# Keys of two context chunks in one matmul of 500 columns, and new fill tables for the prologue and the last batch

## The chip, the cores and the metric

The kernel runs on one core of a Trainium2 chip, as one launch. The metric is the device time in microseconds, median of several runs. Engines are named as in the profile: PE is TensorE, ACT is ScalarE, DVE is VectorE, POOL is GpSimd, SP is SyncE, which issues most DMAs.

## The reference

```python
def xattn(query, key, value, Wq, Wk, Wv, Wo):      # 16 heads of 32
    q = (query @ Wq.T).reshape(B, L, H, D) * scale
    k = (key @ Wk.T).reshape(B, -1, H, D)
    v = (value @ Wv.T).reshape(B, -1, H, D)
    scores = sigmoid(einsum('blhd,bshd->bhls', q, k))
    o = einsum('bhls,bshd->blhd', scores, v).reshape(B, L, E)
    return o @ Wo.T

x = x + tanh(g_xattn) * xattn(layernorm(x), ctx, ctx, ...)    # x (16, 224, 512), ctx (16, 750, 512)
x = x + tanh(g_ffn) * ffn(layernorm(x), w1, b1, w2, b2)       # 8 experts of 2048, gelu, 448 tokens each
```

## The kernel before, in words

**Arithmetic.** Every large product is made of three products of split operands: an operand is stored as a high part (HI, rounded to the matmul's format) and a low part (LO, the rest), and `three_terms` adds HI·HI, HI·LO and LO·HI over four blocks of 128 rows. One fill is therefore 12 matmuls into one PSUM bank. ACT makes the HI part, DVE the LO part.

**Batches.** `batches` runs the body for b = -1 (prologue), 0 to 15 (the 16 batches) and 16 (tail); all are unrolled. A body has 12 steps s. In step s PE computes the scores of step s (`scores`: 8 matmuls of 224 columns, a head group of four heads mt = s // 3 against a third of the context s % 3), ACT turns them into `probs` by one sigmoid, and PE meanwhile does the fills that the table of this batch lists for this step. `scores_ps` is single, so the scores of step s+1 wait for the sigmoid of step s. Twice a batch, at steps 0 and 6, `heads` multiplies six steps of probabilities by the values (48 short matmuls).

**Fills** have a kind and a number. K: keys of context chunk c = j % 3 for head group j // 3, where j = (i + 6) % 12 is the step that will use them; 250 columns. V: values, 512 columns. Q: queries, 224 columns. O: output projection, 512 columns. U and T: transposes. S: transpose of the layernorm moments into a row. The tables are `FILL` (batches 1 to 14), `FILL_FIRST` (prologue), `FILL_0` (batch 0) and `FILL_LAST` (batch 15). All engines walk the same table: PE fills the bank, ACT and DVE take it out (`leave`), POOL stores K, Q, U and S results to DRAM scratch in table order. Fill number g of a table uses bank g % 3 of `fill_ps` and waits until the fill that held that bank has left it.

**Keys and queries** go through DRAM to be laid out again: `store_k` writes one K fill (250 KB) to `k_scr`, a ring of six places with a semaphore `s_k_st` for each, and `gather_k(n, j)` on SP reads it back in three DMAs into one of three places of `k_st`, two steps ahead, once the scores of step j-3 are done. The same holds for `store_q` and `gather_q`.

**SP is one queue** and each of its waits holds everything behind it. Two places matter here. At the prologue's end `load_xT(1)` waits for the stored row of moments (`s_stat_st`) and then reads it back as `x_mr`; `gather_k(0, 2)` stands behind it. In the last batch, at step 5, `load_w1(0, 1)` loads the second piece of the first expert's weights into `k_stage` (the buffer from which `store_k` writes) and waits for that until all keys are stored; `gather_k` for step 8 stands behind it.

```python
if known(e, 0) and c == 1:
    for r in range(RING):
        alone(sp, s_k_st[r], 16 * 2 * B)
```

**Last batch.** No later batch has to be prepared, so `HIDDEN_AT` puts the first expert's hidden products (`hidden`, in halves of 6 matmuls of 448 columns) into the steps from 8 on; its numbers count steps of batch 15, and 12 is step 0 of the tail. After the tail's `heads` come the two O fills, into `scores_ps`.

**Experts.** After the tail, 8 experts of 8 chunks run in `expert`; the change touches nothing in them.

Of the kernel before, what the change touches and what calls it, by code (L numbers as in the profile page):

```python
# [10 lines left out]
F32 = mybir.dt.float32  # L11
# [25 lines left out]
def flamingo_block(nc, io, scr, out):  # L37
# [27 lines left out]
    FILL = [(1, "K", 0), (1, "O", 0), (2, "K", 1), (2, "O", 1), (3, "K", 2), (3, "V", 2), (3, "U", 0), (3, "U", 1),  # L65
# [3 lines left out]
    FILL_FIRST = [(0, "K", 6), (1, "T", 0), (1, "T", 1), (2, "Q", 0), (3, "Q", 1), (4, "K", 7), (5, "K", 8), (6, "K", 9),  # L69
                  (7, "V", 0), (8, "K", 10), (9, "K", 11), (9, "S", 1)]  # L70
    FILL_0 = [(0, "Q", 6), (0, "Q", 7), (1, "K", 0), (1, "V", 7), (2, "K", 1), (2, "V", 2), (3, "K", 2),
              (3, "V", 3), (4, "K", 3), (4, "V", 4), (5, "V", 5)] + [f for f in FILL if f[0] > 5]
    FILL_LAST = [(0, "K", 0), (0, "K", 1), (1, "K", 2), (1, "O", 0), (1, "V", 2), (2, "K", 3), (2, "V", 3),
                 (3, "K", 4), (3, "V", 4), (4, "V", 5), (5, "O", 1), (7, "K", 5), (8, "S", 0), (9, "U", 0), (10, "U", 1)]
# [47 lines left out]
    def nth(kind, b, i):  # L122

        if kind == "K":
            return K_FIRST[i] if known(b, -1) else STEPS * b + AHEAD + i + 1
        if kind == "S":
            return 1 if i == 1 else b + 2
        return {"V": 6, "Q": KT, "T": 2, "O": 2, "U": 2}[kind] * target(b, kind, i) + tile_of(kind, i) + 1

    def tile_of(kind, i):  # L130

        return i % KT if kind == "Q" else i % 6 if kind == "V" else i

# [49 lines left out]
    with ExitStack() as ctx:  # L183
# [133 lines left out]
        def _(sp):  # L317
# [107 lines left out]
            def load_w1(e, c):  # L425
# [82 lines left out]
        def _(pool):  # L508
# [14 lines left out]
            def store_k(b, i):  # L523
# [3 lines left out]
                at(pool, s_k_in[(j - RING) % 3], 16 * COPIES * (4 * n + (j - RING) // 3 + 1))  # L527
                own(pool)
                pool.dma_start(scr["k"][j % RING].rearrange("h p s -> p h s"), k_stage[:, j % 3].bitcast(F32)  # L529
                               ).then_inc(s_k_st[j % RING], 16)  # L530
# [25 lines left out]
            for r in range(RING):  # L556
                pool.wait_ge(s_k_st[r], 16 * 2 * B)
# [5 lines left out]
        def _(pe):  # L563
# [61 lines left out]
            def fill(b, kind, i):  # L625
# [149 lines left out]
        def _(act):  # L775
            def ctx_hi(n, h, par, c):
                act.wait_ge(s_ctx_in[chunk_place(par, c)], 16 * (chunk_round(h, par, c) + 1))

                at(act, full["K"], STEPS * (n - 1) + 9 + c + 1)
# [26 lines left out]
            def leave(b, kind, i):  # L806
# [9 lines left out]
                elif kind == "K":  # L816
                    j = step_of(i)
                    at(act, s_k_st[(j - 3) % RING], 16 * (2 * n + (j - 3) // RING + 1))
                    nc.scalar.copy(k_stage[:, j % 3, HI, :], ps[:, 0:SC]).then_inc(hi["K"], 1)  # L819
# [25 lines left out]
            def body(b, h, par):  # L845
                nh, npar = (h, 1) if par == 0 else (h + 1, 0)
                for s in range(STEPS):
# [26 lines left out]
                    if known(b, B - 1):  # L874
# [4 lines left out]
                        if s == 8:  # L879
# [18 lines left out]
            def e_hi(e, m, c):  # L898
# [335 lines left out]
```

## Time and profile before

| | us |
|---|---|
| median of 3 runs | 1717.65 (1716.29 to 1717.78) |
| profiled execution, its own time | 1717.5 |
| its span in the trace | 1716.0 |
| PE busy | 1690.3 (99%), 12525 matmuls |
| ACT busy | 777.0 (45%) |
| DVE busy | 682.3 (40%) |
| POOL busy | 210.2 (12%) |
| DMA engines, mean busy share | 63% of the span |

A matmul's duration in the trace overlaps with the next one's; what a fill costs PE is the distance from its start to the start of what follows. The profiled execution lies 0.15 us under the median. Its own time is 1.5 us more than its span.

### The profile page before, as it was taken

The page shows a single profiled execution, that of the slowest core. Times are in us where ns is not written, and L with a number is a line of the kernel's source. Part 1 is how long each engine was busy: PE and PEld are TensorE (multiplying, and loading weights), DVE is VectorE, ACT ScalarE, POOL GpSimd, SP SyncE. Part 2 cuts the span into 40 slices and gives each one's busy share as a digit, 9 for nine tenths or more (in the row PEclk, how much of TensorE's full clock was granted, in tenths as well). Part 3 has the DMA queues.
Part 4 walks back from the last instruction along what each step waited for, and adds up shares of the span by engine and source line. Part 5 has one row for each costly group of instructions (what it writes and reads, how often), then busy time and mean ns, then how long its engine had stood idle before and what let it go on. Part 6 is the DMA issues. An engine that isn't in the chain of part 4 may idle for free. (4 is left out here: it accounts for less than half of the span.)

```text
span 1716.0 us, 32304 instructions
## 1 busy us (share of the span) xinstructions
PE 1690.3 (99%) x12525; PEld 1510.3 (88%) x12525; DVE 682.3 (40%) x1139; ACT 777.0 (45%) x975; POOL 210.2 (12%) x303
## 2 busy tenths in 40 slices
PE   8999999999999999999999996999999999999999
PEld 7888888888888888898888885899999999999998
DVE  5323322332332232233233223355556464555554
ACT  4545555545555545455455443434333333333332
POOL 1122122122122121122121120000000000000000
PEclk9999999999999999999999998999999999999999
DMA  7887687686687686787786683545263535435351
GB/s 243 232 235 206 186 236 202 180 236 196 190 237 201 193 237 201 199 230 190 202 233 190 197 226 101 159 139 191 104 206 107 183 130 165 154 117 186 101 175 59
DMA packets 199651, 315.53 MB, mean 184 GB/s; under 512 B 25368, under 2 KB 152672, under 8 KB 199520
## 3 DMA queue, kind: packets, MB, share of 16 engines
q1 hardware_dynamic: 176176, 236.05, 49.5%
q0 software_dynamic: 23344, 77.68, 13.0%
q8 instruction: 88, 1.44, 0.4%
q14 instruction: 43, 0.35, 0.1%
HBM read 235.06 MB, written 78.58 MB: 183 GB/s over the span
## 5 line engine op out<-in xcount | busy, mean ns | idle before, releaser
L795 ACT ACTIVATE probs<-scores_ps 125x1792 f32<-125x1792 f32 x192 | 320.4, 1669 | 152.4 <-PE scores_ps L602 122.4
L756 PE MATMUL scores_ps<-ctx_hl,wK 128*128 128x448 f32 x1536 | 316.7, 362 | 0.4 <-ACT st_row L826 0.4
L756 PEld LDWEIGHTS scores_ps<-ctx_hl,wK 128*128 128x128 f32 x1536 | 288.0, 188 | 20.4 <-issue 0.6
L570 PE MATMUL fill_ps<-ctx_hl,wK 128*128 128x250 f32 x2304 | 297.9, 281 | 1.0 <-DVE wK L955 1.0
L570 PEld LDWEIGHTS fill_ps<-ctx_hl,wK 128*128 128x128 f32 x2304 | 280.0, 189 | 7.0 <-issue 5.7
L570 PE MATMUL fill_ps<-wV,ctx_hl 128*125 128x512 f32 x1152 | 281.1, 395 | 0.0
L570 PEld LDWEIGHTS fill_ps<-wV,ctx_hl 128*125 128x125 f32 x1152 | 207.9, 185 | 46.6
L736 PE MATMUL fill_ps<-wQ,wV 128*128 128x448 f32 x1152 | 245.7, 368 | 0.4 <-DVE wV L1109 0.4
L529 POOL DMA_DIRECT2D k_scr<-k_stage x192 | 139.2, 725 | 792.1 <-DVE k_stage L1037 597.5
L736 PEld LDWEIGHTS fill_ps<-wQ,wV 128*128 128x128 f32 x1152 | 217.5, 189 | 18.1 <-DVE wV L1109 0.6
L602 PEld LDWEIGHTS scores_ps<-q_st,k_st 96*125 96x125 f32 x1536 | 191.9, 190 | 30.2 <-DMA k_st<-k_scr 13.9
L602 PE MATMUL scores_ps<-q_st,k_st 96*125 96x224 f32 x1536 | 203.2, 275 | 14.2 <-DMA k_st<-k_scr 13.4
L1037 DVE TENSOR_TENSOR k_stage<-fill_ps,k_stage 128x250 fp32r<-128x250 f32 x192 | 79.9, 416 | 287.5 <-ACT k_stage L819 286.8
L619 PE MATMUL heads_ps<-probs,v_sb 125*32 125x224 f32 x3072 | 151.9, 353 | 0.0
L843 ACT COPY v_sb<-fill_ps 125x512 f32<-125x512 f32 x96 | 56.3, 586 | 195.1 <-PE fill_ps L570 195.1
L619 PEld LDWEIGHTS heads_ps<-probs,v_sb 125*32 125x32 f32 x3072 | 96.6, 110 | 45.5 <-issue 0.3
L924 ACT ACTIVATE q_stage<-fill_ps,b_sb 128x448 f32<-128x448 f32 x96 | 60.8, 635 | 143.1 <-PE fill_ps L736 143.0
L949 DVE TENSOR_TENSOR ctx_hl<-ctx_raw,ctx_hl 128x1000 fp32r<-128x1000 f32 x48 | 57.6, 1200 | 165.7 <-ACT ctx_hl L781 165.7
L1120 DVE CAST ctx_hl<-q_stage 128x896 fp32r<-128x896 f32 x64 | 40.1, 627 | 162.4 <-ACT q_stage L924 162.4
L570 PE MATMUL fill_ps<-xnT,wQ 128*128 128x224 f32 x768 | 96.6, 279 | 0.2 <-DVE wQ L955 0.2
L570 PEld LDWEIGHTS fill_ps<-xnT,wQ 128*128 128x128 f32 x768 | 91.8, 195 | 0.7 <-DVE wQ L955 0.4
L819 ACT CAST k_stage<-fill_ps 128x250 fp32r<-128x250 f32 x192 | 69.8, 363 | 41.3 <-PE fill_ps L570 41.3
(85 smaller groups left out, 1274.0 us busy)
## 6 DMA issues: line engine op xcount, KB each, us to landing
k_st<-k_scr SPq DMA_DIRECT2D x576, 125.0 KB, 3.8
v_sb<-w_in SPq DMA_DIRECT2D x94, 512.0 KB, 4.5
k_scr<-k_stage POOLq DMA_DIRECT2D x192, 250.0 KB, 4.7
ctx_raw<-ctxT_in SPq DMA_DIRECT2D x48, 500.0 KB, 5.7
q_st<-q_scr SPq DMA_DIRECT2D x192, 112.0 KB, 3.4
probs<-w_in SPq DMA_DIRECT2D x32, 512.0 KB, 3.8
x_res<-x_in SPq DMA_DIRECT2D x32, 448.0 KB, 4.3
q_scr<-q_stage POOLq DMA_DIRECT2D x64, 224.0 KB, 5.6
```

The source lines that it names most:

```text
L529: pool.dma_start(scr["k"][j % RING].rearrange("h p s -> p h s"), k_stage[:, j % 3].bitcast(F32)).then_inc(s_k_st[j % RING], 16)
L570: last = pe.matmul(out_, lhsT(kt, a), rhs(kt, c), start=(kt == 0 and t == 0), stop=(kt == KT - 1 and t == 2))
L602: last = pe.matmul(scores_ps[0:ST, j, t * L:(t + 1) * L], k_st3[:, r, j, t * ST:(t + 1) * ST], q_st3[:, slot, j, :], start=True, stop=True)
L619: last = pe.matmul(heads_ps[j * HD:(j + 1) * HD, cols], v_sb[0:ST, v_place(par, 2 * pair + t), mt * P + j * HD:mt * P + (j + 1) * HD], pro ...
L736: last = pe.matmul(hid_ps[bank][:, 0:T], w1[:, slot, a, kt, k * P:(k + 1) * P], xt[:, d, kt, :], start=(kt == 0 and t == 0), stop=(kt == K ...
L756: last = pe.matmul(y_ps[:, dt, 0:T], w2[:, slot, a, k, dt * P:(dt + 1) * P], hid_hl[:, slot, d, k, :], start=(c == 0 and k == 0 and t == 0 ...
L795: nc.scalar.activation(probs[0:ST, s % VISIT], scores_ps[0:ST, :, 0:2 * L], ACT.Sigmoid, scale=SCALE).then_inc(s_probs, 1)
L819: nc.scalar.copy(k_stage[:, j % 3, HI, :], ps[:, 0:SC]).then_inc(hi["K"], 1)
L843: nc.scalar.copy(v_sb[0:ST, v_place(1 - par if i < 2 else par, i % 6), :], fill_bank(b, "V", i)[0:ST, :]).then_inc(done["V"], 1)
L924: nc.scalar.activation(hid[:, k, :], hid_ps[2 * (c % 2) + k][:, 0:T], ACT.Gelu_apprx_tanh, bias=b1[:, 2 * c + k:2 * c + k + 1]).then_inc(s ...
L949: nc.vector.tensor_tensor(ctx_chunk(c, LO), ctx_raw[:, chunk_place(par, c)], ctx_chunk(c, HI).bitcast(F32), ALU.subtract).then_inc(s_ctx_l ...
L1037: nc.vector.tensor_tensor(k_stage[:, j, LO, :], ps[:, 0:SC], k_stage[:, j, HI, :].bitcast(F32), ALU.subtract).then_inc(done["K"], 1)
```

## The change

1. `is_pair(b, i)`: from batch 0 on, a K fill with i % 3 == 0 covers chunks 0 and 1 of the context for its head group. Its 12 matmuls have 500 columns: the moving operand is read in two pieces of 250 that lie 2000 elements apart, and 2000 bytes of a bank are written in one piece. One ACT cast and one DVE subtraction take 500 columns out, and one POOL DMA of 500 KB stores both ring places. Fills with i % 3 == 1 are gone (except K 7 and K 10 in the prologue, which keeps single fills); chunk 2 keeps its own fill of 250 columns.
2. A pair's store signals only the semaphore of its first ring place; `ring_sem` and `keys_done` give the new numbers. A pair's store waits for the gathers from both places that it overwrites.
3. K 5 moves from step 7 to 6, K 8 from 9 to 8, and with them the splitting of the next context's chunks (`CTX_SPLITS`) from steps 5, 6, 7 to 4, 5, 7.
4. The two Q fills of batch 0, step 0, move into the prologue, step 9, ahead of S.
5. In the last batch `load_w1(0, 1)` goes to `ctx_raw` and waits for the split tokens (`s_xt_lo`) instead of the keys. Its split moves from step 8 to 7. O 1 moves from step 5 to 3, K 5 from 7 to 6, S from 8 to 9, U 0 and U 1 from 9 and 10 to 8 and 9, and the hidden halves start at step 7.

```diff
-    FILL = [(1, "K", 0), (1, "O", 0), (2, "K", 1), (2, "O", 1), (3, "K", 2), (3, "V", 2), (3, "U", 0), (3, "U", 1),
-            (4, "K", 3), (4, "V", 3), (5, "V", 4), (5, "V", 5), (6, "K", 4), (7, "K", 5), (7, "K", 6), (7, "Q", 0),
-            (8, "K", 7), (8, "V", 0), (9, "K", 8), (9, "K", 9), (9, "S", 0), (9, "Q", 1), (10, "K", 10), (10, "V", 1),
-            (11, "K", 11), (11, "Q", 2), (11, "Q", 3)]
+    FILL = [(1, "K", 0), (1, "O", 0), (2, "O", 1), (3, "K", 2), (3, "V", 2), (3, "U", 0), (3, "U", 1), (4, "K", 3),
+            (4, "V", 3), (5, "V", 4), (5, "V", 5), (6, "K", 5), (7, "K", 6), (7, "Q", 0), (8, "K", 8), (8, "V", 0),
+            (9, "K", 9), (9, "S", 0), (9, "Q", 1), (10, "V", 1), (11, "K", 11), (11, "Q", 2), (11, "Q", 3)]
...
-                  (7, "V", 0), (8, "K", 10), (9, "K", 11), (9, "S", 1)]
...
+                  (7, "V", 0), (8, "K", 10), (9, "K", 11), (9, "Q", 2), (9, "Q", 3),
+                  (9, "S", 1)]
...
-    FILL_LAST = [(0, "K", 0), (0, "K", 1), (1, "K", 2), (1, "O", 0), (1, "V", 2), (2, "K", 3), (2, "V", 3),
-                 (3, "K", 4), (3, "V", 4), (4, "V", 5), (5, "O", 1), (7, "K", 5), (8, "S", 0), (9, "U", 0), (10, "U", 1)]
...
+    FILL_LAST = [(0, "K", 0), (1, "K", 2), (1, "O", 0), (2, "V", 2), (3, "K", 3), (3, "O", 1),
+                 (3, "V", 3), (4, "V", 4), (5, "V", 5), (6, "K", 5), (8, "U", 0), (9, "U", 1), (9, "S", 0)]
...
-    CTX_SPLITS = {5: 0, 6: 1, 7: 2}
...
-    HIDDEN_AT = {8: [(0, 0, 0), (0, 0, 1)], 9: [(0, 1, 0)], 10: [(0, 1, 1)], 11: [(1, 0, 0)], 12: [(1, 0, 1)]}
+    CTX_SPLITS = {4: 0, 5: 1, 7: 2}
...
+    HIDDEN_AT = {7: [(0, 0, 0)], 8: [(0, 0, 1)], 9: [(0, 1, 0)], 10: [(0, 1, 1)], 11: [(1, 0, 0), (1, 0, 1)]}
...
+    def is_pair(b, i):
+        return b > -1 and i % 3 == 0
...
+    def ring_sem(n, j):
+        return j % RING if n == 0 and j < AHEAD else j % RING - (j % 3 == 1)
...
-                return x_raw[:, 0:HALF] if c == 0 else k_stage[:].rearrange("p r h s -> p (r h s)")[:, 0:HALF].bitcast(F32)
+                return x_raw[:, 0:HALF] if c == 0 else ctx_raw[:].rearrange("p r s -> p (r s)")[:, 0:HALF]
...
                 if known(e, 0) and c == 1:
-                    for r in range(RING):
-                        alone(sp, s_k_st[r], 16 * 2 * B)
+                    alone(sp, s_xt_lo, 2)
...
+                at(pool, s_k_in[(j + 1 - RING) % 3], 16 * COPIES * (4 * n + (j + 1 - RING) // 3 + 1))
                 own(pool)
-                pool.dma_start(scr["k"][j % RING].rearrange("h p s -> p h s"), k_stage[:, j % 3].bitcast(F32)
-                               ).then_inc(s_k_st[j % RING], 16)
+                pool.dma_start(scr["k"][j % RING:j % RING + 2].rearrange("r h p s -> p (r h) s"),
+                               k_stage[:, 0:2].rearrange("p r h s -> p (r h) s").bitcast(F32)
+                               ).then_inc(s_k_st[ring_sem(n, j)], 16)
...
+                    if is_pair(b, i):
+                        last = three_terms(ps[:, 0:2 * SC], lambda kt, a: w["K"][:, a, kt, mt * P:(mt + 1) * P],
+                                           lambda kt, a: ctx_hl[:, 0:2, a, kt, :])
...
-                        if s == 8:
+                        if s == 7:
                             e_hi(0, 1, 1)
```

**PE where batch 0 begins.** S of the prologue is the row with `mv`. Before:

```order
L570 MATMUL fill_ps<-ctx_hl,wK 128x250 x24
L674 MATMUL fill_ps<-ident,mv 8x112
L602 MATMUL scores_ps<-q_st,k_st 125x224 x8
L570 MATMUL fill_ps<-xnT,wQ 128x224 x24
L602 MATMUL scores_ps<-q_st,k_st 125x224 x8
L570 MATMUL fill_ps<-ctx_hl,wK 128x250 x12
L570 MATMUL fill_ps<-wV,ctx_hl 125x512 x12
L602 MATMUL scores_ps<-q_st,k_st 125x224 x8
```

Changed:

```order
L589 MATMUL fill_ps<-xnT,wQ 128x224 x24
L697 MATMUL fill_ps<-ident,mv 8x112
L621 MATMUL scores_ps<-q_st,k_st 125x224 x8
L589 MATMUL fill_ps<-wV,ctx_hl 125x512 x12
L621 MATMUL scores_ps<-q_st,k_st 125x224 x8
L589 MATMUL fill_ps<-ctx_hl,wK 128x500 x12
L621 MATMUL scores_ps<-q_st,k_st 125x224 x8
```

The queries now stand ahead of S; between S and the scores of step 2 (the third row of scores) there is one V fill and one pair, where two Q, one K and one V fill stood.

**POOL at the same place**, the stores of the prologue. Before:

```order
L529 DMA k_scr<-k_stage 128x2x250 [waits done_K]
L520 DMA q_scr<-q_stage 128x2x224 [waits done_Q] x2
L529 DMA k_scr<-k_stage 128x2x250 [waits done_K] x5
L545 DMA stat_scr<-st_row 4x2x112 [waits done_S]
L520 DMA q_scr<-q_stage 128x2x224 [waits done_Q] x2
```

Changed:

```order
L542 DMA k_scr<-k_stage 128x2x250 [waits done_K]
L532 DMA q_scr<-q_stage 128x2x224 [waits done_Q] x2
L542 DMA k_scr<-k_stage 128x2x250 [waits done_K] x5
L532 DMA q_scr<-q_stage 128x2x224 [waits done_Q] x2
L564 DMA stat_scr<-st_row 4x2x112 [waits done_S]
```

The two query stores now stand between the last key store and the store of the moments.

**PE in the changed last batch**, from the scores of step 7 to the end of its `heads`; `x_res` is U and `mv` is S:

```order
L621 MATMUL scores_ps<-q_st,k_st 125x224 x8
L759 MATMUL fill_ps<-wQ,wV 128x448 x6
L621 MATMUL scores_ps<-q_st,k_st 125x224 x8
L701 MATMUL fill_ps<-ident,x_res 128x112 x4
L759 MATMUL fill_ps<-wQ,wV 128x448 x6
L621 MATMUL scores_ps<-q_st,k_st 125x224 x8
L701 MATMUL fill_ps<-ident,x_res 128x112 x4
L697 MATMUL fill_ps<-ident,mv 8x112
L759 MATMUL fill_ps<-wQ,wV 128x448 x6
L621 MATMUL scores_ps<-q_st,k_st 125x224 x8
L759 MATMUL fill_ps<-wQ,wV 128x448 x6
L621 MATMUL scores_ps<-q_st,k_st 125x224 x8
```

U 1 and S now stand in one step, next to each other, and both use bank 2; before, S, U 0 and U 1 had a step each (8, 9 and 10).

## Rows read from the trace of the kernel before

**Rows 1.** Whom PE waited for: total us, times, longest us.
```profile
PE scores_ps L602 <- DMA k_st<-k_scr: 13.4, 1, 13.4
PE fill_ps L674 <- DVE mv L31: 3.3, 1, 3.3
```

**Rows 2.** Stretches: length, then each engine's busy us, PE clock, DMA share, GB/s.
```profile
35.00:41.60 6.60, 6.60 (x34) 6.56 (x35) 0.67 (x2) 3.64 (x5) 1.91 (x3) 0.54 0.30 95
...
229.39:294.96 65.57, 65.57 (x588) 57.27 (x587) 20.32 (x45) 33.92 (x43) 12.78 (x18) 1.00 0.73 209
...
1016.27:1093.08 76.81, 62.62 (x576) 51.05 (x574) 17.98 (x35) 32.81 (x36) 6.98 (x10) 0.89 0.50 132
```

**Rows 3.** PE in order of time, batch 2: start us, us, what, count.
```profile
205.05 2.94 PE L570 MATMUL fill_ps<-ctx_hl,wK 128*128 128x250 f32 x24
207.83 1.50 PE L570 MATMUL fill_ps<-xnT,wQ 128*128 128x224 f32 x12
209.16 1.04 PE L602 MATMUL scores_ps<-q_st,k_st 96*125 96x224 f32 x8
210.04 1.57 PE L570 MATMUL fill_ps<-ctx_hl,wK 128*128 128x250 f32 x12
211.44 2.94 PE L570 MATMUL fill_ps<-wV,ctx_hl 128*125 128x512 f32 x12
214.22 1.03 PE L602 MATMUL scores_ps<-q_st,k_st 96*125 96x224 f32 x8
```

**Rows 4.** The chain that ended last, experts: start us, us, matmuls of 448 columns.
```profile
1142.18 4.81 PE scores_ps L756 x24
```

**Rows 5.** Last batch, SP's queue and PE in order of time, [idle before <- releaser].
```profile
1066.10 0.35 SPq L436 DMA_DIRECT2D k_stage<-w_in  x1
1066.60 1.27 SPq L333 DMA_DIRECT2D k_st<-k_scr  x3
...
1072.38 2.02 PE L602 MATMUL scores_ps<-q_st,k_st 96*125 96x224 f32 x8 [13.37 <-DMA k_st<-k_scr]
...
1081.71 1.11 PE L602 MATMUL scores_ps<-q_st,k_st 96*125 96x224 f32 x8 [0.23 <-ACT probs L795]
...
1084.67 1.11 PE L602 MATMUL scores_ps<-q_st,k_st 96*125 96x224 f32 x8 [0.23 <-ACT probs L795]
...
1086.93 4.75 PE L619 MATMUL heads_ps<-probs,v_sb 125*32 125x224 f32 x96
...
1093.08 5.76 PE L570 MATMUL scores_ps<-wO,oT 128*112 128x512 f32 x24
```

**Rows 6.** ACT between the sigmoids of steps 9, 10 and 11 of the last batch.
```profile
1082.86 1.67 ACT L795 ACTIVATE probs<-scores_ps 125x1792 f32<-125x1792 f32 x1 [0.87 <-PE scores_ps L602]
1084.42 0.53 ACT L836 COPY x_raw<-fill_ps 128x448 f32<-128x448 f32 x1
```

**Rows 7.** Prologue's end, PE in order of time.
```profile
34.98 0.34 PE L674 MATMUL fill_ps<-ident,mv 112*8 112x112 f32 x1 [3.35 <-DVE mv L31]
...
36.89 4.85 PE L570 MATMUL fill_ps<-xnT,wQ 128*128 128x224 f32 x24
```

**Rows 8.** Prologue's end, DVE, POOL, SP's queue and PE's weight loads in order of time.
```profile
34.86 0.42 DVE L1037 TENSOR_TENSOR k_stage<-fill_ps,k_stage 128x250 fp32r<-128x250 f32 x1
...
36.55 0.61 POOL L545 DMA_DIRECT2D stat_scr<-st_row  x1
...
39.49 0.83 SPq L392 DMA_DIRECT2D x_mr<-stat_scr  x2
...
40.41 1.33 SPq L333 DMA_DIRECT2D k_st<-k_scr  x3
...
46.70 0.95 PEld L602 LDWEIGHTS scores_ps<-q_st,k_st 96*125 96x125 f32 x8 [0.34 <-DMA k_st<-k_scr]
```

**Rows 9.** Issue to landing of those three gathers, and of batch 3's store of moments.
```profile
DMA to landing us min/median/max: 4.3/4.5/5.4
...
DMA to landing us min/median/max: 4.2/4.2/4.2
```

More of the change, by code:

```diff
@@ L124, in nth @@
         if kind == "K":
-            return K_FIRST[i] if known(b, -1) else STEPS * b + AHEAD + i + 1
+            return K_FIRST[i] if known(b, -1) else K_FILLS * b + AHEAD + i - (i + 1) // 3 + 1
         if kind == "S":
@@ L527, in store_k @@
                 at(pool, s_k_in[(j - RING) % 3], 16 * COPIES * (4 * n + (j - RING) // 3 + 1))
+                if not is_pair(b, i):
+                    own(pool)
+                    pool.dma_start(scr["k"][j % RING].rearrange("h p s -> p h s"), k_stage[:, j % 3].bitcast(F32)
+                                   ).then_inc(s_k_st[ring_sem(n, j)], 16)
+                    return
+                at(pool, s_k_in[(j + 1 - RING) % 3], 16 * COPIES * (4 * n + (j + 1 - RING) // 3 + 1))
                 own(pool)
[L529 to L530 removed]
+                pool.dma_start(scr["k"][j % RING:j % RING + 2].rearrange("r h p s -> p (r h) s"),
+                               k_stage[:, 0:2].rearrange("p r h s -> p (r h) s").bitcast(F32)
+                               ).then_inc(s_k_st[ring_sem(n, j)], 16)
             def body(b, h, par):
@@ L556, in _ @@
             for r in range(RING):
-                pool.wait_ge(s_k_st[r], 16 * 2 * B)
+                pool.wait_ge(s_k_st[r], 16 if r % 3 == 1 else 16 * 2 * B)
             for mt in range(KT):
@@ L817, in leave @@
                     j = step_of(i)
-                    at(act, s_k_st[(j - 3) % RING], 16 * (2 * n + (j - 3) // RING + 1))
-                    nc.scalar.copy(k_stage[:, j % 3, HI, :], ps[:, 0:SC]).then_inc(hi["K"], 1)
+                    last = 2 * n + (j - 3) // RING + 1
+                    if last > 0:
+                        m, k = (n, j - 3) if j > 2 else (n - 1, j - 3 + STEPS)
+                        act.wait_ge(s_k_st[ring_sem(m, k)], 16 * last)
+                        if is_pair(b, i) and ring_sem(m, k + 1) != ring_sem(m, k):
+                            act.wait_ge(s_k_st[ring_sem(m, k + 1)], 16 * last)
+                    if is_pair(b, i):
+                        nc.scalar.copy(k_stage[:, 0:2, HI, :], ps[:, 0:2 * SC].rearrange("p (r s) -> p r s", s=SC)
+                                       ).then_inc(hi["K"], 1)
+                    else:
+                        nc.scalar.copy(k_stage[:, j % 3, HI, :], ps[:, 0:SC]).then_inc(hi["K"], 1)
                 elif kind == "Q":
@@ L902, in e_hi @@
                 if known(e, 0) and c == 0:
-                    act.wait_ge(full["V"] if m == 1 else full["K"], (6 if m == 1 else 12) * B)
+                    act.wait_ge(full["V"] if m == 1 else full["K"], 6 * B if m == 1 else keys_done(B - 1, STEPS - 1))
                 if m == 1:
@@ L1036, in leave @@
                     j = step_of(i) % 3
-                    nc.vector.tensor_tensor(k_stage[:, j, LO, :], ps[:, 0:SC], k_stage[:, j, HI, :].bitcast(F32),
-                                            ALU.subtract).then_inc(done["K"], 1)
+                    if is_pair(b, i):
+                        nc.vector.tensor_tensor(k_stage[:, 0:2, LO, :], ps[:, 0:2 * SC].rearrange("p (r s) -> p r s", s=SC),
+                                                k_stage[:, 0:2, HI, :].bitcast(F32), ALU.subtract).then_inc(done["K"], 1)
+                    else:
+                        nc.vector.tensor_tensor(k_stage[:, j, LO, :], ps[:, 0:SC], k_stage[:, j, HI, :].bitcast(F32),
+                                                ALU.subtract).then_inc(done["K"], 1)
                 elif kind == "Q":
@@ L1117, in split_hidden @@
                 if known(e, 0) and c == 0:
-                    dve.wait_ge(full["K"], 12 * B)
+                    dve.wait_ge(full["K"], keys_done(B - 1, STEPS - 1))
                     dve.wait_ge(full["V"], 6 * B)
```

21 lines of the change are left out of this document (13 added, 8 removed).

## The prediction, made before the changed kernel ran

> **What bounds the kernel now.** I read the busy times first (the table above): PE is busy in 99% of the span, no other engine in half of it. Then the waits of PE [rows 1]: in the whole span it waits for little else than two things, once 13.4 us for gathered keys and once 3.3 us for the moments. Then the stretches [rows 2]. An ordinary batch lasts 65.57 us and PE is busy in all 65.57 of it, at full clock. So an ordinary batch gets shorter only if the matmuls themselves cost less; what ACT, DVE, POOL and the DMA queues save there is worth nothing unless it was late. The first and the last batch are different: there the clock column falls to 0.54 and 0.89, the two waits lie there, and the order of SP's and POOL's queues sets the time. I price the three places apart.
>
> **Ordinary batches: the pair.** Starts to starts in batch 2 [rows 3]: 24 key matmuls of 250 columns in 207.83 - 205.05 = 2.78 us; 12 alone in 211.44 - 210.04 = 1.40; 12 value matmuls of 512 columns in 214.22 - 211.44 = 2.78, so 232 ns each. In the experts 24 matmuls of 448 columns take 4.81 us [rows 4], 200 ns each. No row has 500 columns. 500 columns at the full 2.4 GHz are 208 ns. What a matmul takes over its columns is 14 ns at 448 (200 - 187), 19 at 512 (232 - 213) and 12 to 13 at 250. So 500 columns should take 222 to 227 ns; I take 224, nearer to the 448 row, since keys are multiplied as the experts' weights are, with 128 stationary columns. A pair then takes 12 x 224 = 2.69 us, where two fills took 2.78 (together) to 2.80 (apart, and a little more where other work stands between). I take a gain of 0.12 us a pair, between 0.05 and 0.17. There are 4 pairs in each of batches 0 to 14, without the first of batch 0, which goes into the prologue's sum: 59 x 0.12 = **7.1 us less** (3 to 10).
>
> What no row shows is a moving operand read in two pieces, and what that costs. Bounded from above by the price of two separate starts: then a pair is as dear as 24 matmuls in 2.78 and the gain is nearly nil. From below by columns alone, 12 x 208 = 2.50 us, a gain of 0.3 a pair or 18 us. I stay at 0.12, since the break comes once in 250 columns.
>
> The Trainium skill (TensorE: Matmul & The Clock Gate, Back-to-back issue gap) gives N/2.4 + 2.5 ns for a warm matmul. By it a pair would save only 12 x 2.5 ns = 0.03 us, and all pairs 1.8 us. The rows disagree with the page: 232 ns at 512 columns, not 216 [rows 3].
>
> What else moves in an ordinary batch I cost at nothing. Steps 2 and 10 keep one fill of 2.78 us; the sigmoid loop needs scores start to scores start 2.96 us (1084.67 - 1081.71, where it did bind) [rows 5], and 0.87 + 2.78 = 3.65 covers it. ACT's and DVE's 500 columns lie beside the next fill. The cover of the bigger store is the two steps between a store and its gather, over 7 us. The context split starts a step earlier, behind the two chunks' last K fill, which is now at step 4; it lies beside the 5.6 us of two V fills. The Q fills and S keep their places. If this cover failed, a late gather would show as a PE wait for `k_st` in every batch; 1.1 us a batch would eat all gain outside the prologue.
>
> **Last batch.** Here one wait sets the time. SP stood at the load into `k_stage` until 1066.10, and the gather for step 8 was issued behind it at 1066.60 [rows 5]. PE waited 13.37 us, then ran at half clock for some time: step 8's scores at 1072.38 took 2.02 us, not 1.03. From this batch's first scores to the O fills of the tail is 1093.08 - 1016.27 = 76.8 us.
>
> The changed load waits for the split tokens, which come before step 5's scores, so SP issues it at once and the next gather as soon as its slot is free. I built the new row of work from the same prices: heads 4.67 + 0.1, V, O 2.78 each, pair 2.69, K 1.40 to 1.53, scores 0.87 to 0.97. Step 0: 8.4 us; 1: 5.0; 2: 3.7; 3: 9.1; 4: 3.7, and 0.5 of wait, because the cast of the tokens again stands ahead of sigmoid 4; 5: 3.7; 6: 7.1. So step 7's scores start 41.2 us after the first. Steps 7 and 8 have less work than the sigmoid loop and cost 2.96 each. Step 9 has a **new wait**: U 1 and S are neighbours and use the same bank, so S waits until ACT has taken U 1 out, and ACT does that after sigmoid 9. From the scores' start: sigmoid starts after 1.15, takes 1.6, U's copy 0.53 [rows 6], so S starts at 3.3, and the hidden half behind it ends at 4.7, not 2.6. Step 9 costs 4.7, step 10 2.96, step 11 0.9 + 2 x 1.25 = 3.4. That is 41.2 + 5.9 + 4.7 + 3.0 + 3.4 = 58.2 to `heads`, and from `heads` to the O fills 1093.08 - 1086.93 = 6.15 as before (no hidden half covers the split of the last outputs now, but its own 1.5 us is gone too). 64.4 against 76.8: **12.4 us less**. The tail behind it starts from the same events and keeps its length. Bounds: 14.5 without the new wait and the one at step 5; 11 if the last keys (K 5, stored about 1.5 us after their fill, landing some 3 us later, gathered in 5) come 1.5 us late for step 11, which by my row of work they just do not.
>
> **Prologue.** Before, PE stood 3.35 us ahead of S [rows 7] and ran the next 6 us at half clock (0.54 [rows 2]): the two Q fills of batch 0 took 4.7 us where 24 such matmuls take 2 x 1.33 = 2.7 [rows 3, 7]. The change puts these Q fills into the gap. S now waits for the bank of K 11, whose subtract ends at 34.86 + 0.42 = 35.28 [rows 8], so S comes 0.3 us later, at about 35.4, but after an idle of 1.1 us, not 3.35. If that were all, 1.4 + 2.7 + 3 us of half clock would mean 5 to 6 us less.
>
> But step 2's scores did not wait for PE even before: the weight load at 46.70 is marked as waiting for the gather [rows 8]. That gather is behind `x_mr` on SP, which is behind the stored moments: stored at 36.55, `x_mr` at 39.49, gather at 40.41, landed at 46.70 [rows 8]. In POOL's new order the two query stores (0.73 each) come ahead of the moments: 36.55 + 1.5 = 38.0. Their landing took 2.9 us alone (39.49 - 36.55) and 4.2 beside key and query stores [rows 9]; now it has 700 KB of stores ahead of it, so I take 4.2: `x_mr` at 42.3, the gather at 43.2, its third DMA 0.9 later and 5.4 us to land [rows 9]: step 2's scores at **48.9** (47.2 to 49.6), 2.2 us later than before. PE reaches this point, with one V fill and one pair since S, at 35.4 + 0.9 + 2.8 + 0.1 + 0.9 + 2.7 = 42.9. It then stands 6 us, longer than the 3.35 that were followed by the low clock before, so I expect the same again: half of some 6 us, 3 us lost. Ahead of 48.9 PE has done one K fill more than before (1.4 us), and the gather of step 3, a step behind on SP, comes perhaps 0.5 late. The sum is 2.2 - 1.4 + 3.0 + 0.5, less about 0.8 because part of the half clock falls on PE's waits for the sigmoid: **3.5 us more** (1.6 less to 6 more).
>
> **Sum.** 1717.5 - 7.1 - 12.4 + 3.5 = 1701.5, against its own 1717.5; the profiled run is 0.15 from the median, which I let go. Experts: the same work, no change.
>
> **Rivals.**
> (a) *The prologue is really mended*: the moments land in 2.9 us and the gather in 4, or the stall comes without low clock. Then the prologue gives 1 to 5 us instead of costing 3.5: 1693 to 1697. For it: the first gather there landed in 4.3. Against: the gather was already late by 0.34 [rows 8].
> (b) *Pairs bring nothing*, since a matmul's extra time grows with its columns (12 ns at 250, 19 at 512): then only the last batch counts, 1717.5 - 1.8 - 12.4 + 3.5 = 1707.
> (c) *Slower*: the moving operand in two pieces is read more slowly, as a stall of the array at each break. The place is every pair fill. It decides from 8.9 / (59 x 12) = 12.6 ns over the 234 of two separate matmuls, so from 247 ns for 500 columns; at 265 ns, 30 ns above that price a matmul, it is 1717.5 - 8.9 + 59 x 12 x 0.031 = 1731. For it: no row of this trace reads so. Against it: within a piece the columns are neighbours as before, and only one step in 500 is long. The Trainium skill (SBUF — State Buffer, Door 1: The DMA port swizzle) says that an access which crosses to a new line of 16 bytes pays; by that one long step costs what a quarter of all steps cost anyway, and (c) would not happen.
> (d) *The last batch keeps part of its wait*, because something else on SP is late there, the keys of K 5 or the first expert's tokens: 5 to 8 us of the 12.4 stay, 1707 to 1710.
>
> **How the numbers follow.** Forecast as summed (1698 to 1704): 0.55. (a) 0.15, (b) 0.12, (c) 0.07, (d) 0.11. The bounds of the terms give 1717.5 - 10 - 14.5 - 1.6 = 1691 at one end and 1717.5 - 3 - 11 + 6 = 1709.5 at the other; joint extremes are rare. From 1693 to 1710 all of the forecast and nearly all of (a), (b) and (d) lie inside. A difference under 0.2% (3.4 us) can't be told from none. Above 1721 lies most of (c), 0.06; between 1714 and 1721 the rest of (c) and a sum of bad ends of (d), 0.03; below is 0.91.
>
> **What would show it.** In the trace of the changed kernel: 12 key matmuls of 500 columns from start to start 2.69 us (2.78 or more is (b), 2.97 or more is (c)); an ordinary batch of 65.1 us; in the last batch no wait above 2 us, one of about 2 us before S in step 9, and full clock throughout; from its first scores to the tail's O fills 64 us; in the prologue a wait of 4 to 6 us for `k_st` ahead of step 2's scores, then a stretch at half clock, with `x_mr` issued after 41. I would be wrong in kind if PE waited for `k_st` in ordinary batches, or if the experts changed.

## The result, and the profile of the changed kernel

The changed kernel takes 1748.95 us (median of 4 runs, 1745.25 to 1753.60), the kernel before 1716.99 (4 runs). The ratio is 1.0186, with a 95% interval from 1.0166 to 1.0206: 32 us slower, where 16 us faster was forecast. The profiled execution took 1751.64 us with a span of 1749.8, 33.8 more than the span before.

What PE waits for, in the changed kernel (engine, tile and line, releaser, us in total, times, longest):

```profile
PE fill_ps L589 <- DVE ctx_hl L982: 27.2, 15, 1.8
PE scores_ps L621 <- DMA k_st<-k_scr: 5.0, 1, 5.0
PE fill_ps L697 <- ACT x_raw L869: 1.8, 1, 1.8
PE scores_ps L621 <- ACT probs L819: 1.8, 4, 0.6
...
PE scores_ps L589 <- DVE oT L1055: 1.4, 1, 1.4
```

The first row has no counterpart in [rows 1]. It stands in each of 15 batches, and it is no gather: PE waits for the low part of the next context. Here are two of the fifteen on PE's timeline, in two different batches (start us, us, then in brackets the idle time before and its releaser):

```profile
80.44 1.04 PE L621 MATMUL scores_ps<-q_st,k_st 96*125 96x224 f32 x8
83.29 1.64 PE L589 MATMUL fill_ps<-ctx_hl,wK 128*128 128x250 f32 x12 [1.81 <-DVE ctx_hl L982]
84.77 2.94 PE L589 MATMUL fill_ps<-wV,ctx_hl 128*125 128x512 f32 x12
87.55 1.03 PE L621 MATMUL scores_ps<-q_st,k_st 96*125 96x224 f32 x8
...
488.83 1.04 PE L621 MATMUL scores_ps<-q_st,k_st 96*125 96x224 f32 x8
491.68 2.67 PE L589 MATMUL fill_ps<-ctx_hl,wK 128*128 128x250 f32 x12 [1.81 <-DVE ctx_hl L982]
494.15 3.50 PE L589 MATMUL fill_ps<-wV,ctx_hl 128*125 128x512 f32 x12
497.48 1.04 PE L621 MATMUL scores_ps<-q_st,k_st 96*125 96x224 f32 x8
```

The waits are equal, what follows is not. Behind the first, the K fill takes 1.48 us from start to start and the V fill 2.78. Behind the second they take 2.47 and 3.33: the granted clock had fallen to its lower level, 1.2 GHz, and this costs 1.5 us more. It happened in 9 of the 15 batches.

The fill at 83.29 is K 8, the keys of the third context chunk of the **next** batch for head group 0; the first fill that reads a chunk waits for its split into HI and LO. That chunk was split by ACT (80.89) and DVE (81.94), ahead of the sigmoid of this step:

```profile
80.89 1.03 ACT L805 CAST ctx_hl<-ctx_raw 128x1000 fp32r<-128x1000 f32 x1
81.81 1.67 ACT L819 ACTIVATE probs<-scores_ps 125x1792 f32<-125x1792 f32 x1
```
```profile
81.94 1.20 DVE L982 TENSOR_TENSOR ctx_hl<-ctx_raw,ctx_hl 128x1000 fp32r<-128x1000 f32 x1 [0.53 <-ACT ctx_hl L805]
```

In the kernel before, the same split stood at the same place, and K 8 (the first 12 of the 24 matmuls) came 3.2 us after its end, behind K 7, V 0 and the scores of step 9 [rows 3]:

```profile
210.66 1.20 DVE L949 TENSOR_TENSOR ctx_hl<-ctx_raw,ctx_hl 128x1000 fp32r<-128x1000 f32 x1 [0.53 <-ACT ctx_hl L781]
```
```profile
215.09 2.97 PE L570 MATMUL fill_ps<-ctx_hl,wK 128*128 128x250 f32 x24
```

The stretches (from, to, length, busy time and count of PE, PEld, DVE, ACT, POOL, granted clock, DMA share, GB/s) are a batch with a fall of the clock, a batch without one, and everything from the O fills of the tail to the end. Under them the same last stretch of the kernel before:

```profile
102.17:171.03 68.86, 67.05 (x539) 56.52 (x538) 19.89 (x42) 33.95 (x39) 9.98 (x14) 0.98 0.72 199
171.03:238.34 67.31, 65.50 (x538) 55.02 (x538) 19.89 (x41) 33.96 (x39) 9.97 (x14) 1.00 0.73 204
1121.62:1749.80 628.18, 624.23 (x3069) 574.31 (x3069) 339.43 (x385) 217.83 (x269) 4.95 (x9) 1.00 0.44 145
```
```profile
1093.08:1716.00 622.92, 618.82 (x3070) 574.59 (x3069) 339.28 (x385) 217.93 (x269) 4.91 (x9) 1.00 0.45 146
```

[rows 2] had 65.57 us for a batch and 76.81 for the last. The last batch, from its first scores to the O fills, is now 1121.62 - 1057.24 = 64.38 us:

```profile
1057.24 1.03 PE L621 MATMUL scores_ps<-q_st,k_st 96*125 96x224 f32 x8
...
1107.80 0.26 PE L697 MATMUL fill_ps<-ident,mv 112*8 112x112 f32 x1 [1.79 <-ACT x_raw L869]
...
1121.62 3.70 PE L589 MATMUL scores_ps<-wO,oT 128*112 128x512 f32 x15 [1.40 <-DVE oT L1055]
```

**Where the 33.8 us came from**, by marks that both traces have. From the start to the `heads` of batch 0, step 6: 69.32, before 66.82, +2.5 (with one K fill of 1.4 us more done by then). From there to the last batch's first scores: 987.92, before 949.45, +38.5. The last batch: -12.4. From the O fills on: +5.3. The sum is 33.8 before rounding.

The 5.3 us at the end are not the change's. The experts' code is the same, and its hidden matmuls take 206.7 ns from start to start in this execution against 202.6 in the profile of before, at the same clock. Of the 13 profiles here eleven have 202.6, those of experiments 4 and 5 too, which only put work into the waits of the changed kernel, and two have 206.7, this one and that of experiment 9. The 29 executions of the kernel before lie in two groups, 17 from 1715.79 to 1717.87 us and 12 from 1719.03 to 1723.21. A difference of less than that needs several runs or a look at one place of the trace, and I compare places below.

### The profile page after: what moved, and what is told of

Same layout as the page of the kernel before. It is cut to its first block and busy times, and to the rows that moved or that the text cites. A ratio compares the mean times of both kernels' runs of the same rounds, so it can differ in the third digit from the quotient of the medians.

```text
span 1749.8 us, 30424 instructions
## 1 busy us (share of the span) xinstructions
PE 1704.0 (97%) x11781; PEld 1484.2 (85%) x11781; DVE 675.3 (39%) x1077; ACT 777.8 (44%) x913; POOL 166.9 (10%) x241
## 5 line engine op out<-in xcount | busy, mean ns | idle before, releaser
L589 PE MATMUL fill_ps<-ctx_hl,wK 128*128 128x500 f32 (+1 forms) x1560 | 299.0, 343 | 27.7 <-DVE ctx_hl L982 27.2
L589 PEld LDWEIGHTS fill_ps<-ctx_hl,wK 128*128 128x128 f32 x1560 | 243.9, 197 | 61.0 <-issue 35.6
L589 PE MATMUL fill_ps<-wV,ctx_hl 128*125 128x512 f32 x1152 | 286.0, 400 | 0.0
L589 PEld LDWEIGHTS fill_ps<-wV,ctx_hl 128*125 128x125 f32 x1152 | 213.9, 190 | 48.8
L1071 DVE TENSOR_TENSOR k_stage<-fill_ps,k_stage 128x500 fp32r<-128x500 f32 x62 | 42.1, 678 | 234.0 <-ACT k_stage L849 234.0
L542 POOL DMA_DIRECT2D k_scr<-k_stage x68 | 48.9, 719 | 516.6 <-DVE k_stage L1074 428.1
L589 PE MATMUL fill_ps<-wO,oT 128*112 128x512 f32 x360 | 88.0, 393 | 0.0
```

The lines of the kernel that those rows point to most:

```text
L589: last = pe.matmul(out_, lhsT(kt, a), rhs(kt, c), start=(kt == 0 and t == 0), stop=(kt == KT - 1 and t == 2))
L1071: nc.vector.tensor_tensor(k_stage[:, 0:2, LO, :], ps[:, 0:2 * SC].rearrange("p (r s) -> p r s", s=SC), k_stage[:, 0:2, HI, :].bitcast(F32) ...
```

## Experiments

The kernel before was run again beside each round of experiments, and the ratios are to these runs: its median was 1721.34 us (9 runs) for experiments 1, 4, 8 and 10, 1719.03 (9 runs) for 2, 6, 7 and 9, and 1717.12 (7 runs) for 3, 5 and 11. Differences between medians of different rounds are therefore rough.

**1. K 8 back at step 9**, all else as changed. The theory: the move of K 8 alone, and not pairs, stores or gathers, made the kernel slower.

```diff
-(7, "Q", 0), (8, "K", 8), (8, "V", 0), (9, "K", 9)
+(7, "Q", 0), (8, "V", 0), (9, "K", 8), (9, "K", 9)
```

> The changed kernel with one entry of FILL moved back: K 8 from step 8 to step 9, behind the split of the next context's third chunk at step 7, which it reads. Theory: the 15 waits of 1.8 us for that split, and the nine falls of the clock behind them, go; ordinary batches become 65.4 us (65.58 less four pairs at 0.05) and the median 1749 - 28.7 - 13.9 = 1706. If the slower hidden matmuls of the experts (39.04 us for half an expert, 38.68 in the kernel before) are a state of the run and not of the program, 1701. Rival, the larger stores delay something in ordinary batches: a batch stays over 66.5 us and the median above 1720.

Measured: 1704.79 us (4 runs; ratio to before 0.9908, 0.9876 to 0.9941), 44 us under the changed kernel. No wait for `ctx_hl` is left, and a batch is 65.22 us with PE busy in all of it:

```profile
101.07:166.29 65.22, 65.22 (x538) 54.93 (x537) 19.89 (x42) 33.87 (x39) 10.01 (x15) 1.00 0.77 210
```

Against the batches above this is 2.09 us for a wait of 1.81 and what it adds around it (15 batches: 31.3), and 1.54 more for each of 9 falls (13.9): 45.2 us for one entry of a table. Less the gain of the pairs, 5.2 us (below), and less 1.4, since the changed kernel had done one more K fill at the first mark, these are the 38.5 us between the marks, within 0.1.

**2. The split one step earlier, K 8 left at step 8.** The theory says that K 8 may stand at step 8 if its operand is there.

```diff
-    CTX_SPLITS = {4: 0, 5: 1, 7: 2}
+    CTX_SPLITS = {4: 0, 5: 1, 6: 2}
...
-                    if attends(b) and prepares(b) and s in (1, 2, 6):
-                        load_ctx(b + 1, nh, npar, {1: 0, 2: 1, 6: 2}[s])
+                    if attends(b) and prepares(b) and s in (1, 2, 5):
+                        load_ctx(b + 1, nh, npar, {1: 0, 2: 1, 5: 2}[s])
```

> The changed kernel with K 8 left at step 8, but the next context's third chunk loaded one step earlier (behind step 5 in place of 6) and split one step earlier (6 in place of 7). Theory (the 15 waits of 1.8 us for DVE ctx_hl and the falls of the clock behind them are the split's being one step late for K 8, and nothing else about the move): waits and falls gone, ordinary batches at 65.2 us, 1704 to 1706, as with K 8 at step 9. Rival (loading and splitting a step earlier meets the V fills' leaves or the chunk's buffer, and another wait takes its place): ordinary batches at 66 us or more, 1716 or above.

Measured: 1702.65 us (3 runs; 0.9908, 0.9881 to 0.9934). The batch, the split on DVE, and K 8 on PE with no idle time before it:

```profile
99.19:164.44 65.25, 65.25 (x538) 54.92 (x537) 19.89 (x42) 33.85 (x39) 9.98 (x14) 1.00 0.78 209
```
```profile
76.04 1.20 DVE L982 TENSOR_TENSOR ctx_hl<-ctx_raw,ctx_hl 128x1000 fp32r<-128x1000 f32 x1 [0.51 <-ACT ctx_hl L805]
```
```profile
80.35 1.56 PE L589 MATMUL fill_ps<-ctx_hl,wK 128*128 128x250 f32 x12
```

The split ends at 77.24, 3.1 us ahead of the fill. So the step at which the next context is split was the cause, and there was room to have it earlier.

**3. K 8 at step 8 in the kernel before**, and nothing else. Does the early K 8 cost as much without pairs?

```diff
-            (8, "K", 7), (8, "V", 0), (9, "K", 8), (9, "K", 9)
+            (8, "K", 7), (8, "K", 8), (8, "V", 0), (9, "K", 9)
```

> The kernel before with one edit: K 8 is done at step 8 behind K 7, not at step 9. Nothing else of the change is in it: no pairs, the old last batch and prologue. Theory (the loss of the changed kernel comes from K 8 alone, which reads the next context's third chunk a step before its split): PE waits 1 to 2 us for DVE ctx_hl in each of 15 batches, and the granted clock falls in some of them: 1717 + 15 to 27 for the waits, + up to 14 for the falls: 1735 to 1758. Rival (the wait needs the pairs or their new order of copies): no wait for ctx_hl, 1717 to 1722.

Measured: 1726.41 us (2 runs; 1.0053, 1.0033 to 1.0073), 9.3 above before, less than the theory expected. Its waits, and PE's timeline in batch 0:

```profile
PE fill_ps L570 <- DVE ctx_hl L949: 6.2, 15, 0.4
```
```profile
78.07 1.56 PE L570 MATMUL fill_ps<-ctx_hl,wK 128*128 128x250 f32 x12
80.05 1.63 PE L570 MATMUL fill_ps<-ctx_hl,wK 128*128 128x250 f32 x12 [0.41 <-DVE ctx_hl L949]
```

The wait is there in 15 batches, but of 0.4 us, since K 7 (78.07, 1.4 us) stands ahead of K 8 in the same step and covers the rest; the batch is 66.18 us and its clock never fell. The pair had taken K 7 out of step 8. So both parts of the change meet here: one brought K 8 forward, the other removed the work that would have hidden its wait. The expectation had missed this cover too.

**4 and 5. PE kept busy in the wait.** Is the fall of the clock caused by PE standing still? The changed kernel gets transposes of the identity (results unused) ahead of each K 8, first 13, then 5. They only fill the waiting for the operand: the batches keep their length (below).

```diff
+                        if not known(b, -1) and (kind, i) == ("K", 8):
+                            pe.wait_ge(s_o_lo, 2 * b + 1)
+                            turns(13)
```

> The changed kernel with 13 transposes of the identity on PE right ahead of each K 8 fill, in place of idling there; their result is used by nothing. Theory: the clock falls only because PE idles, so no fall is left in ordinary batches, the waits stay hidden behind the dummies, which must not be longer than the wait, and the median is 1749 - 14 = 1735. Rival, the clock falls for another reason (power, the DMA load): the falls stay and the median is 1749 or more.

> The changed kernel with 5 transposes of the identity ahead of each K 8, where an earlier kernel had 13. With 13, 0.4 us of each wait of 1.8 us were left as idle time, the clock never fell in an ordinary batch and the time was 1733.7 us; with none, 1.8 us were left, the clock fell in 9 of 15 batches and the time was 1749. With 5 about 1.3 us should be left. Theory (what makes the clock fall is how long PE stands): fewer falls than 9 or none: 1734 to 1744. Rival (any break at this place lets it fall, and the 13 transposes hid it otherwise): 9 falls or so, 1749.

With 13 the idle time left is 0.4 us in each batch, and the time 1733.72 us (2 runs). With 5 it is 1.26 us, and the time 1734.82 (2 runs). PE's timeline with 5:

```profile
81.65 0.71 PE L731 MATMUL heads_ps<-ident 128*128 128x128 f32 x5
83.62 1.64 PE L589 MATMUL fill_ps<-ctx_hl,wK 128*128 128x250 f32 x12 [1.26 <-DVE ctx_hl L985]
```

In neither did the clock fall in an ordinary batch; all their batches are 67.3 us, the length of the changed kernel's six batches without a fall. So 1.26 us of idle time left the clock up in all 15 batches, and 1.81 us did not in 9 of 15. The executions without a profile agree by their mean granted clock: 0.988 or 0.989 in all four of the changed kernel, 0.997 or 0.998 in all four of these two. The falls cost 1749 - 1734 = 15 us by the medians, and 9 x 1.54 = 13.9 by the batches. Why six of the fifteen were spared, with the same wait, stays open.

**6. Both chunks of a pair in one piece.** `ctx_hl` is laid out so that the 500 columns of the moving operand are neighbours; K 8 at step 9.

```diff
-        ctx_hl = sb("ctx_hl", [P, 3, 2, KT, SC], F32R)
+        ctx_hl = sb("ctx_hl", [P, 2, KT, 3, SC], F32R)
...
-                                           lambda kt, a: ctx_hl[:, 0:2, a, kt, :])
+                                           lambda kt, a: ctx_hl[:, a, kt, 0:2, :].rearrange("p c s -> p (c s)"))
```

> The kernel with K 8 back at step 9 (1704.8 us), with the split context laid out so that the two chunks of a fill of 500 columns lie in one piece (the moving operand has one run of 500 numbers, not two of 250 that are 2000 numbers apart). In that kernel's profile a fill of two chunks takes 2.75 us (229 ns a matmul) where 500/512 of the 232.5 ns of the 512-column matmuls would be 227. Theory (the break costs next to nothing): 2.75 us a pair still, time within 2 us. Rival (the break in the operand eats the gain): 2.69 us a pair, 59 x 0.06 = 3.5 us lower, 1701.

Measured: 1701.22 us (2 runs; 0.9896, 0.9860 to 0.9931). PE around a pair, in the kernel of experiment 1 and in this one:

```profile
498.04 2.91 PE L589 MATMUL fill_ps<-ctx_hl,wK 128*128 128x500 f32 x12
500.79 2.94 PE L589 MATMUL fill_ps<-wO,oT 128*112 128x512 f32 x12
```
```profile
494.79 2.88 PE L589 MATMUL fill_ps<-ctx_hl,wK 128*128 128x500 f32 x12
497.51 2.93 PE L589 MATMUL fill_ps<-wO,oT 128*112 128x512 f32 x12
```

A pair goes from 2.75 to 2.72 us, and a batch from 65.22 to 65.09:

```profile
98.58:163.67 65.09, 65.09 (x539) 54.95 (x538) 19.89 (x42) 33.84 (x39) 9.98 (x14) 1.00 0.77 210
```

Neither expectation is met exactly. The break costs 2 to 3 ns a matmul, 2 us in all batches, which is real in the trace and too small for two runs to show.

**7. The last batch's change alone, in the kernel before**: single K fills, old prologue. Against the kernel of experiment 8, which differs only in the pairs, it prices the pairs.

```diff
-                    for r in range(RING):
-                        alone(sp, s_k_st[r], 16 * 2 * B)
+                    alone(sp, s_xt_lo, 2)
```

(and `FILL_LAST`, `HIDDEN_AT`, the place in `ctx_raw` and the split at step 7, as in the change.)

> The kernel before with the last batch's change alone (S behind U 1 one step earlier, the first keys' load no longer behind the second half-batch, the new list of fills), its keys in single fills of 250 columns as before and its prologue as before. It does all that the kernel with the old prologue and K 8 at step 9 does (1702.8 us, span 1698.3), but for the pairs. Theory (last batch -12.4 us, a pair worth 0.05 us in its fill and the batch 0.35 us in all): 1717.5 - 12.4 = 1705, that is 3 to 6 us above the kernel with pairs. Rival (pairs are worth the 0.12 us of the prediction): 1709 to 1710. Rival (the last batch's gain needs the pairs): 1712 or more.

Measured: 1710.63 us (5 runs; 0.9952, 0.9936 to 0.9968). Its last batch runs from 1017.03 to 1083.03, 66.0 us with one fall of the clock in it, against 76.81 [rows 2]: this part stands on its own. Its ordinary batch is 65.56 us, as before. The kernel with pairs is 7.9 us faster by the medians, more than the 3 to 6 expected, and 7.6 by the profiled spans. 15 x 0.35 = 5.2 of that are the batches, 0.087 us a pair, as the theory had it; the rest, 2.4 us, isn't the price of the pairs in the fills. 0.9 of it stands already ahead of S (34.95 against 34.08), where the two kernels are the same. Most of the other 1.5 lies in batch 0, where in this execution step 2's scores waited 1.9 us for `k_st` with single fills and not at all with a pair in its place; no run takes that apart.

**8. The old prologue** with pairs and K 8 at step 9: the two Q fills stay in batch 0.

```diff
-    ... (9, "K", 11), (9, "Q", 2), (9, "Q", 3), (9, "S", 1)]
+    ... (9, "K", 11), (9, "S", 1)]
```

> e1 with the prologue of the kernel before: two Q fills back in batch 0, step 0, and S directly behind K 11. Theory of the prediction: the new order delays the moments and with them the gather for step 2 and costs 1 to 3.5 us, so this is 1 to 3.5 us faster than e1; in the trace the wait of 5 us for k_st goes and one of 3.3 us for the moments returns. Rival, the new prologue gains: this is 2 to 5 us slower than e1.

Measured: 1702.78 us (4 runs; 0.9899, 0.9872 to 0.9927), 2.0 under experiment 1. In the profiles the `heads` of batch 0, step 6, start at 66.81 with the old prologue; with the new one at 67.87 to 70.29 in the eight kernels that have it. Part of that is the start of the program, which differs between executions before the two orders part. Counted from one of the first transposes (14.32 to 15.77 us), the new order loses 0.6 to 3.7 us against the old one with a pair in it (experiments 8 and 11). The sign is shown, by traces and not by the medians, whose runs overlap (1699.26 to 1705.44 and 1699.71 to 1709.04).

**9. The moments stored ahead of the queries** in the new prologue. By the prediction the gather for step 2 is late because `x_mr` stands ahead of it on SP.

```diff
+                todo = fills(b)
+                if known(b, -1):
+                    todo = [f for f in todo if f[1:] not in (("Q", 2), ("Q", 3))] + [(9, "Q", 2), (9, "Q", 3)]
-                for _, kind, i in fills(b):
+                for _, kind, i in todo:
```

> The kernel with K 8 back at step 9 (1704.8 us, span 1701.8), and in the prologue GpSimd stores the projection's moments of S ahead of the queries' Q 2 and Q 3. In that kernel's profile step 2's scores stand at 47.4 us behind 3.1 us of waiting for DMA k_st, at half clock. Theory (x_mr goes out late because S's leave stands behind two query stores on GpSimd's queue, and the keys' load stands behind x_mr): step 2's scores start 0.5 to 1.5 us earlier, the wait for k_st shrinks from 3.1 to about 2, the time is 1 to 3 us lower: 1702 to 1704. Rival (the keys' own chain of leave, store and load sets step 2, whatever x_mr does): scores at 47.4 us as now, 1704.8, no difference.

SP's queue and the scores of step 2:

```profile
38.19 0.84 SPq L405 DMA_DIRECT2D x_mr<-stat_scr  x2
39.13 1.33 SPq L346 DMA_DIRECT2D k_st<-k_scr  x3
```
```profile
46.53 2.02 PE L624 MATMUL scores_ps<-q_st,k_st 96*125 96x224 f32 x8 [4.37 <-DMA k_st<-k_scr]
```

`x_mr` is issued 3.65 us after S's start, not 5.5 as in the changed kernel, and the gather right behind it, but the scores start 12.0 us after S (12.6 in the changed kernel, 11.9 and 12.0 in experiments 2 and 6). The gather issued earlier took longer: 7.4 us from its issue at 39.13 to the scores, against 6.2 in the changed kernel. The wait is 4.37 us and did not shrink to 2. The median is 1702.29 us (4 runs; 0.9900, 0.9879 to 0.9921) and the scores come at 46.53; both would fit the theory, but experiments 6 and 2, whose moments are stored behind the queries, have such scores too (46.43 and 46.98), and the median is 2.5 under experiment 1 with the runs of both overlapping. The step "SP's order makes the gather late" isn't borne out; what sets the 5.7 to 7.4 us from that gather's issue to its scores, in the eight profiles of the new order, is open.

**10. The load into `k_stage` back**, waiting for the keys, in the kernel of experiment 1.

```diff
-                    alone(sp, s_xt_lo, 2)
+                    for r in range(RING):
+                        alone(sp, s_k_st[r], 16 if r % 3 == 1 else 16 * 2 * B)
```

> e1 with the load of the first expert's second weight piece back in k_stage and waiting for all keys; the rest of the last batch as changed. Theory: the destination and its wait are what cost 13.4 us before; with K 5 a step earlier the load goes out about 4 us after K 5's fill, step 8's scores wait 6 to 8 us and some low clock follows: 7 to 11 us slower than e1. Rival, the new fill order made the gain: within 2 us of e1.

Measured: 1711.59 us (4 runs; 0.9947, 0.9929 to 0.9965), 6.8 above experiment 1, and 9.3 in the profiled spans. The last batch, from its first scores to the O fills, is 75.27 us against 65.80. SP and PE in the last batch:

```profile
1058.86 0.35 SPq L449 DMA_DIRECT2D k_stage<-w_in  x1
1059.36 1.27 SPq L346 DMA_DIRECT2D k_st<-k_scr  x3
```
```profile
1064.47 2.02 PE L622 MATMUL scores_ps<-q_st,k_st 96*125 96x224 f32 x8 [7.87 <-DMA k_st<-k_scr]
```

This is the picture of [rows 5] again, with 7.9 us in place of 13.4; the last keys, for which the load waits, come a step earlier now. The load's wait was the cause, as predicted.

**11. What the experiments point to**: K 8 at step 9, the old prologue, pairs in one piece, and S of the last batch at step 10, one step behind U 1, so that it doesn't meet it in the same bank.

```diff
-                 (3, "V", 3), (4, "V", 4), (5, "V", 5), (6, "K", 5), (8, "U", 0), (9, "U", 1), (9, "S", 0)]
+                 (3, "V", 3), (4, "V", 4), (5, "V", 5), (6, "K", 5), (8, "U", 0), (9, "U", 1), (10, "S", 0)]
```

> What the experiments point to: the changed kernel with K 8 at step 9, the old prologue, the two chunks of a pair in one piece, and in the last batch S at step 10, one step behind U 1, so that it finds its bank free. From the kernel with the first two of these (1702.8 us, span 1698.3): 0.14 us a batch for the one piece, 2 us in all, and 1.8 us for the wait ahead of S: 1699, span 1694.5, and no wait for ACT x_raw. Rival (S at step 10 only moves its wait to sigmoid 10 or the heads): 1700.5 to 1701.

Measured: **1694.90 us** (4 runs, 1694.06 to 1695.03; ratio to before 0.9868, 0.9851 to 0.9884), 22 us under the kernel before and 54 under the changed one. S has no wait left:

```profile
1057.81 1.11 PE L621 MATMUL scores_ps<-q_st,k_st 96*125 96x224 f32 x8 [0.23 <-ACT probs L819]
1058.75 0.26 PE L697 MATMUL fill_ps<-ident,mv 112*8 112x112 f32 x1
```

Its profiled span, 1693.2, is 5.1 under that of experiment 8: 2.0 for the one piece, 1.6 for S, and 1.4 because the clock didn't fall in the last batch. The median lies further under the 1699 expected, which was counted from experiment 8's median of runs from 1699.26 to 1705.44.

## Why the prediction was wrong, by its own steps

**The step that failed** is "What else moves in an ordinary batch I cost at nothing", and in it "The context split starts a step earlier, behind the two chunks' last K fill". Item 3 of the change says that K 8 moves from 9 to 8 and that the splits move from 5, 6, 7 to 4, 5, 7. The last number doesn't move. I had checked the splits against the K fills that must be over before the chunk may be overwritten, and not against the fill that reads the new chunk. K 8 reads chunk 2 of the next context, and step 7's split of it ends after step 8 begins; in the old order K 7, V 0 and the scores of step 9 came ahead of K 8, 5 us of work [rows 3], and hid it. The prediction named what would make it wrong in kind, a wait for `k_st` in ordinary batches. A wait in ordinary batches it was, but for another operand. Its size, 31.3 us of waits, is twice the forecast gain of 16.

**The clock** was priced in the prologue only, where 3.35 us of standing came ahead of the low clock [rows 7]; the new wait of about 2 us in the last batch was forecast at full clock. That a wait of 1.8 us may bring it down was in none of the rivals; it made the missed waits nearly half as dear again (13.9 on 31.3).

**The pair** was sized from 448 and 512 columns: 224 ns, 0.12 us gained a pair, 7.1 us in all. Measured: 228 to 229 ns, 0.087 us, 5.2 us in the 15 batches; the term's range was 3 to 10. In one piece it is 226.5 ns and 0.12 us. That gain is the forecast one with a bit of luck: the pair takes 2.5 ns a matmul more than the 224 I took, and the two fills that it replaces are dearer too, 2.84 us by the length of the batches and not 2.81. The break that I set at nothing took about a quarter of the gain. Rival (c) needed 247 ns and is out, rival (b) too.

**The last batch**: predicted 64.4 us with a new wait of about 2 us ahead of S and full clock. Measured 64.38, a wait of 1.79, full clock. That isn't luck in the sum: step by step the row of work holds to about 0.15 us (41.4 us to step 7's scores against 41.2, and 4.60 for step 9 against 4.7). The full clock was luck: in six of the ten profiles that have this wait the clock fell there (experiment 1: 1.4 us more). Rival (d) is out; experiments 7 and 10 show the cause alone and its return.

**The prologue**: predicted 3.5 us more, scores of step 2 at 48.9 after 6 us of standing, `x_mr` after 41, then half clock. Measured in the changed kernel:

```profile
47.69 2.02 PE L621 MATMUL scores_ps<-q_st,k_st 96*125 96x224 f32 x8 [4.99 <-DMA k_st<-k_scr]
49.51 3.92 PE L589 MATMUL fill_ps<-wV,ctx_hl 128*125 128x512 f32 x12
```
```profile
40.55 0.83 SPq L405 DMA_DIRECT2D x_mr<-stat_scr  x2
```

The scores came 1.2 us earlier than predicted, the wait was 5 us and not 6, and `x_mr` was issued at 40.55, where the sum had 42.3 and the sign named was "after 41"; the half clock behind it came as described. The sum has a slip of its own too: a gather at 43.2, its third DMA 0.9 later and 5.4 to land give 49.5, not 48.9. The net is 2.5 - 1.4 = 1.1 us more than before: sign and symptoms were right in the main, the term was mis-sized, and one reason given for it fell with experiment 9. Rival (a) is out.

The terms as measured, -5.2 - 12.4 + 1.1, give 1701.0 from the profiled 1717.5. Experiments 1 and 2, which only take the overlooked wait away, have 1704.8 and 1702.7, and by their ratios (both 0.9908) 1701.2. So the sum was sound for the steps it held, and lacked one.

## What to carry to other kernels

When work is moved earlier, list the producers of every operand it reads and where each stands after the move; a check that the buffer is free to be overwritten is another question and doesn't answer this one. Where one part of a change takes work out of a step and another moves a reader into it, look at what is first in the step: the work that went may have been the cover. And price a wait on a busy PE with what may follow it: here 2.09 us a batch, and 1.54 more wherever the clock fell.

## What the runs showed of the hardware that I had not expected

- The granted clock fell from 2.4 to 1.2 GHz behind single waits of 1.8 us in an otherwise busy PE, in 9 of 15 places, and in none of 15 behind waits of 1.26 us. In the last batch it fell behind the wait of 1.79 us ahead of S in six profiles of ten. The Trainium skill (TensorE: Matmul & The Clock Gate, A second HAM failure mode: psum-queue depth-cycling) tells of a kernel in which frequent short stops between groups of matmuls made the clock go up and down. These traces show the same behind a single stop in a batch of 67 us, not behind frequent ones.
- A moving operand in two pieces costs 2 to 3 ns a matmul of 500 columns (228.4 against 226.5 ns from start to start, mean of 682 each).
- The experts' hidden matmuls of 448 columns took 202.6 ns from start to start in eleven profiles and 206.7 in two, at the same clock and with the same code of the experts: 38.7 us or 39.04 for half an expert. That it goes by the execution and not by the program is likely, not shown: the profiled run of experiment 9 (206.7) took 1708.01 us and the other three of that kernel 1701.43 to 1702.45, but no kernel was profiled in both.
